# GpSimd's constants beside the last scores, the last batch's output in its own buffer, first weights loaded during the projection

## What is computed

```
x = x + layernorm(attention(layernorm(x)))      # x: 4 batches x 1024 tokens x 256, 16 heads of 16, rope on q and k
x = x + layernorm(moe(layernorm(x)))

attention: softmax(q k^T / 4) v, then out @ Wo.T + bo
moe:       dist = sqrt(max(|xs|^2 + |cent|^2 - 2 xs cent^T, 1e-12))     # 8 experts
           w, sel = top_k(dist, 2); w = softmax(w)
           out = sum over the two of w * ((silu(xs Wg + bg) * (xs W1 + b1)) W2 + b2)
```

## Time and profile before

| | us |
|---|---|
| median of 3 runs | 1444.86 |
| lowest and highest run | 1440.01, 1445.14 |
| profiled execution, its own time | 1442.97 |
| its span in the trace | 1441.1 |
| TensorE busy in the span | 1321.9 (92%) |
| VectorE, ScalarE, GpSimd busy | 1153.6, 942.0, 557.2 |

### The profile page before, as it was taken

The page is one execution under the profiler, slowest core; times in us unless marked ns, Lnnn a source line. Parts: engine busy times, 40 slices in busy tenths (PEclk is TensorE's granted clock), DMA queues, the critical chain, the costliest instruction groups (busy, mean ns, idle before and its releaser), DMA issues.

```text
span 1441.1 us, 27408 instructions
## 1 busy us (share of the span) xinstructions
PE 1321.9 (92%) x9553; PEld 793.2 (55%) x9554; DVE 1153.6 (80%) x1688; ACT 942.0 (65%) x1731; POOL 557.2 (39%) x473
## 2 busy tenths in 40 slices
PE   7999999999999999999999683699999999999980
PEld 4445333333333333333334451599999899899970
DVE  7989999999999999999930668477777667777765
ACT  4531888888888888888887561254555455455445
POOL 5670013040404023040450540355555455555545
PEclk9999999999999999999999885799999999999995
DMA  6875539647665757677225459665565656555646
GB/s 205 238 275 107 121 69 250 162 88 193 115 187 94 205 98 148 148 128 206 81 79 148 84 169 373 254 165 153 151 164 152 215 151 166 153 149 166 192 118 237
DMA packets 132293, 236.27 MB, mean 164 GB/s; under 512 B 56892, under 2 KB 93183, under 8 KB 130400
## 3 DMA queue, kind: packets, MB, share of 16 engines
q1 hardware_dynamic: 116288, 216.32, 53.9%
q0 software_dynamic: 15904, 18.66, 7.9%
HBM read 161.05 MB, written 79.50 MB: 167 GB/s over the span
## 4 chain that ended last, share of the span: by engine, by line
PE 75%; DVE 8%; DMA 6%; issue 4%; ACT 3%; POOL 3%; SPq 1%; POOLq 0%; DVEq 0%; ACTq 0%
PE psum L1601 21%; PE psum L1627 20%; PE psum L1776 15%; PE psum L1794 6%; DMA y_d<-sums,row_of 3%; PE psum L1796 3%; PE psum L1785 3%; PE psum L1613 2%; PE psum L1575 1%; DVE mx L1051 1%; ACT memory L1419 1%; POOL memory L976 1%; PE psum L1561 1%; DMA values<-xn_d,token_of 1%; PE psum L1758 1%
## 5 line engine op out<-in xcount | busy, mean ns | idle before, releaser
L1051 DVE TENSOR_REDUCE mx<-psum 128x1 f32<-128x1024 f32 x512 | 622.7, 1222 | 13.7 <-PE psum L1601 8.6
L1413 ACT ACTIVATE memory<-psum 128x512 f32<-128x512 f32 x1024 | 553.4, 600 | 63.9 <-PE psum L1613 1.4
L1613 PE MATMUL psum<-stack 50*128 50x512 f32 x1024 | 375.7, 446 | 0.0
L1601 PE MATMUL psum<-stack 48*128 48x512 f32 x1024 | 371.1, 443 | 2.5 <-DVE mx L1051 1.7
L1627 PE MATMUL psum<-memory,values 128*32 128x256 f32 x4096 | 326.3, 391 | 4.6
L1776 PE MATMUL psum<-w_parts,x_parts 128*128 x1278 | 284.8, 376 | 1.2 <-DVE x_parts L1281 1.2
L1601 PEld LDWEIGHTS psum<-stack 48*128 48x128 f32 x1024 | 150.4, 184 | 210.8 <-DVE mx L1051 168.4
L1776 PEld LDWEIGHTS psum<-w_parts,x_parts 128*128 128x128 f32 x1278 | 237.1, 190 | 23.7 <-issue 1.8
L954 POOL DMA_INDIRECT y_d<-sums,row_of x71 | 133.8, 1884 | 179.7 <-DVE sums L1303 149.6
L1490 ACT ACTIVATE sums<-psum,dots 128x256 f32<-128x256 f32 x71 | 33.8, 476 | 233.0 <-issue 118.7
L1627 PEld LDWEIGHTS psum<-memory,values 128*32 128x32 f32 x4096 | 81.9, 108 | 187.8 <-issue 106.6
(11 more groups left out here) (194 smaller groups left out, 1425.7 us busy)
## 6 DMA issues: line engine op xcount, KB each, us to landing
w_parts<-w_d SPq DMA_DIRECT2D x71, 768.0 KB
stack<-qk_scr SPq DMA_DIRECT2D x192, 128.0 KB, 6.0
w_d<-w_parts SPq DMA_DIRECT2D x6, 2736.0 KB, 8.1
w_parts<-w_d SPq DMA_DIRECT2D x6, 2736.0 KB, 14.9
qk_scr<-memory SPq DMA_DIRECT2D x16, 1024.0 KB, 4.5
raw<-in_w SPq DMA_DIRECT2D x16, 684.0 KB
ot_scr<-memory SPq DMA_DIRECT2D x16, 512.0 KB, 3.2
memory<-in_x SPq DMA_DIRECT2D x7, 1024.0 KB, 11.5
```

The costliest lines, as they stand in the source:

```text
L1051: dve.tensor_reduce(mx[:, r, a, t:t + 1], bank(4 + 2 * a, 2), AX, ALU.max, negate=True).then_inc(s_max, 1)
L1413: act.activation(pt[u % 4][:, j, :], bank((c + HG * u + n) % 3), ACT.Exp, scale=SC).then_inc(s_exp, 1)
L1601: ins = pe.matmul(bank(4 + 2 * a + half), qs[t3][at:at + QROWS, r, P * t:P * (t + 1)], ks[t3][at:at + QROWS, r, 512 * half:512 * (half + 1 ...
L1613: pe.matmul(bank((t3 + HG * u + n) % 3), ks[t3][at:at + MROWS, r, P * st:P * (st + 1)], qs[t3][at:at + MROWS, r, 512 * half:512 * (half + ...
```

## The change

- The fourth `ot` buffer. `OT_OF` is gone, each batch has a buffer, and that of batch 3 lies over `o_stage` and `v_stage` and the words behind them. Its loads no longer wait for `s_op`; the first waits until the values have been copied (`s_vg`) and the output is stored.
- SyncE's order. The last output is stored as soon as it is in `o_stage`, its sums are loaded next, then come all loads of batch 2 and batch 3, the latter no longer among the keeps. x2 is stored in four quarters behind keeps 3, 7, 11 and 15.
- The first weights. Load 5 moves into the last attention group, loads 0, 1 and 2 stand behind keeps 5, 9 and 13, each with a wait for the projections that free its place.
- GpSimd. Its constants wait for the weighing of all but the last two units, not for the last store. The halves of `norm_o` of batches 2 and 3 stand alone, before `add_y` 4, 6, 8 and 10, where both halves stood before 6 and 10.
- TensorE waits for the last copy of the output only before `turn_xn2(1)`, which writes the bank that held it.

```diff
--- before.py
+++ after.py
@@ -56,7 +56,6 @@
 Q_PART = [0, 0, 1]
 K_PART = [0, 1, 0]
 HEAD_ORDER = (1, 3, 0, 2)
-OT_OF = (0, 1, 2, 0)
 
 
 def steps(eng, count, stages, head=2):
@@ -188,6 +187,7 @@
         c.at = 16416
         ot = [c.take([2, KC, T]) for _ in range(2 + 1)]
         assert c.at == 24608 + stack_at
+        ot.append(weights[:, c.at:c.at + 2 * KC * T].rearrange("p (a k t) -> p a k t", a=2, k=KC))
         o_stage = c.take([T])
         v_stage = [c.take([ST, HG * D]) for _ in range(2)]
         assert c.at <= 32896
@@ -539,13 +539,11 @@
             sp.wait_ge(s_ot, 16 * HG * (b + 1))
             if b == 2:
                 sp.wait_ge(s_sp, BLOCKS * NG)
-            elif b == 3:
-                sp.wait_ge(s_op, 4)
             src = ot_scr[HG * b:HG * (b + 1), :, :].rearrange("(k x) (j s d) t -> s x j d k t", x=2, s=2, d=D)[0]
             for x in parts:
                 for j in range(HG):
                     at = 64 * x + D * j
-                    sp.dma_start(ot[OT_OF[b]][at:at + D, 0, :, :], src[x, j]).then_inc(s_otl[b % 2], 16)
+                    sp.dma_start(ot[b][at:at + D, 0, :, :], src[x, j]).then_inc(s_otl[b % 2], 16)
 
         def load_sums(sp, b):
 
@@ -563,13 +561,11 @@
             sp.wait_ge(s_rst, 16 * (b + 1))
             if b == 2:
                 sp.wait_ge(s_sp, BLOCKS * NG)
-            elif b == 3:
-                sp.wait_ge(s_op, 4)
             src = r_scr[b].rearrange("(k x j) t -> x j k t", x=2, j=HG)
             for x in parts:
                 for j in range(HG):
                     at = 64 * x + D * j
-                    sp.dma_start(ot[OT_OF[b]][at:at + D, 1, :, :], src[x, j].partition_broadcast(D)).then_inc(s_otl[b % 2], 16)
+                    sp.dma_start(ot[b][at:at + D, 1, :, :], src[x, j].partition_broadcast(D)).then_inc(s_otl[b % 2], 16)
 
         def load_raw(sp, n):
 
@@ -691,39 +687,38 @@
                                  zeros[:, :].rearrange("p (a d) -> p a d", a=1).to_broadcast([P, NT + 1, C])).then_inc(s_yc, 16)
                 elif g == 5:
                     load_wo(sp)
+                elif g == NG - 1:
+                    sp.wait_ge(s_wl, KC * E)
+                    load_w1(sp, 5)
 
             groups(sp, during)
             sp.wait_ge(s_sp, BLOCKS * (NG - 1))
             for m in range(4):
                 sp.dma_start(x2[:, 8 * m:8 * m + 8, :], x_v[:, 8 * m:8 * m + 8, :]).then_inc(s_x2l, 16)
+            store_o(sp, NG - 1)
+            load_sums(sp, B - 1)
             load_ot(sp, 2)
-            store_o(sp, NG - 1)
             load_inverses(sp, 2)
-            load_sums(sp, B - 1)
+            sp.wait_ge(s_vg, NG)
+            load_ot(sp, B - 1)
+            store_inverses(sp, B - 1)
+            load_inverses(sp, B - 1)
             def keep(u):
 
                 sp.wait_ge(s_one, u + 1)
                 sp.dma_start(xn2_d[2 * P * u:2 * P * (u + 1), :].rearrange("(a p) c -> p a c", p=P), xn2[u % 4]).then_inc(s_keep[u % 4], 16)
 
+            x2_kept = x2_d.rearrange("(n p) d -> p n d", p=P)
             for u in range(NT // 2):
-                if u == 2:
-                    store_inverses(sp, B - 1)
                 keep(u)
-                if 2 <= u < 6:
-                    (load_ot, load_inverses)[u // 2 - 1](sp, B - 1, (u % 2,))
-                if u == 7:
-                    sp.wait_ge(s_wl, KC * E)
-                    load_w1(sp, 5)
-                if u == 12:
-                    sp.wait_ge(s_vg, NG)
-                    sp.wait_ge(s_op, 12)
-                    load_w1(sp, 2)
-            sp.wait_ge(s_x2, NT // 2)
-            sp.dma_start(x2_d.rearrange("(n p) d -> p n d", p=P), x2).then_inc(s_x2s, 16)
-            sp.wait_ge(s_op, NT // 2)
-            for n in range(2):
-                load_w1(sp, n)
-            sp.wait_ge(s_x2s, 16)
+                if u % 4 == 3:
+                    sp.wait_ge(s_x2, u + 1)
+                    sp.dma_start(x2_kept[:, 2 * u - 6:2 * u + 2, :], x2[:, 2 * u - 6:2 * u + 2, :]).then_inc(s_x2s, 16)
+                if u in (5, 9, 13):
+                    n = (u - 5) // 4
+                    sp.wait_ge(s_op, 4 * n + 8)
+                    load_w1(sp, n)
+            sp.wait_ge(s_x2s, 64)
             sp.wait_ge(s_dd, 1)
             load_w1(sp, 3)
             sp.wait_ge(s_wc, 1)
@@ -849,11 +844,11 @@
             for r in range(PAIRS):
                 split_max(0, r)
 
-            def norm_o(b):
-
-                for half in range(2):
+            def norm_o(b, halves=(0, 1)):
+
+                for half in halves:
                     pool.wait_ge(s_otl[b % 2], 16 * 4 * HG * (b // 2 + 1))
-                    dims, inverses = [ot[OT_OF[b]][:, part, :, 512 * half:512 * (half + 1)] for part in range(2)]
+                    dims, inverses = [ot[b][:, part, :, 512 * half:512 * (half + 1)] for part in range(2)]
                     pool.tensor_tensor(dims, dims, inverses, ALU.mult).then_inc(s_div, 1)
 
             def split_weights(n):
@@ -885,7 +880,7 @@
             groups(pool, during)
 
 
-            pool.wait_ge(s_ot, 16 * NG)
+            pool.wait_ge(s_pv, UNITS * NG - 2)
             made = [0]
 
             def const(ins):
@@ -927,8 +922,8 @@
                 pool.tensor_tensor(both, both, yn[u % 2], ALU.add).then_inc(s_x2, 1)
 
             for u in range(NT // 2):
-                if u in (6, 10):
-                    norm_o(u // 4 + 1)
+                if u in (4, 6, 8, 10):
+                    norm_o(u // 4 + 1, (u % 4 // 2,))
                 add_y(u)
                 if u >= 3:
                     set_ones(u - 3)
@@ -1686,7 +1681,6 @@
 
 
             pe.wait_ge(s_wo, 48)
-            pe.wait_ge(s_oe, 2 * NG)
             pe.wait_ge(s_exp, BLOCKS * NG)
             pe.wait_ge(s_max, 2 * UNITS * NG)
 
@@ -1704,13 +1698,15 @@
                     dst = bank((4, 5, 0, 1)[u % 4])[:, C * a:C * (a + 1)]
                     pe.matmul(dst, ones_r[:, :], bias_rows, start=True, stop=False)
                     for k in range(KC):
-                        last = pe.matmul(dst, ot[OT_OF[u // 4]][:, 0, k, at + P * a:at + P * (a + 1)], w_o[:, k, :],
+                        last = pe.matmul(dst, ot[u // 4][:, 0, k, at + P * a:at + P * (a + 1)], w_o[:, k, :],
                                          start=False, stop=k == KC - 1)
                 last.then_inc(s_op, 1)
 
             def turn_xn2(u):
                 pe.wait_ge(s_xn2, 2 * u + 2)
                 after(pe, s_xn2t, u - 1)
+                if u == 1:
+                    pe.wait_ge(s_oe, 2 * NG)
                 for a in range(2):
                     for k in range(KC):
                         last = pe.transpose(bank((7, 3)[u % 2])[:, P * (KC * a + k):P * (KC * a + k + 1)],
```

## The result

The changed kernel takes 1446.9 us (median of 20 runs, 1441.31 to 1473.95) where the kernel before takes 1443.3 on the same chip. The ratio is 1.0022, 95% interval 1.0014 to 1.0029: some 3 us slower, by more than the measurement is uncertain, but within the 0.5% that the prediction called no change. It had said 1445.4, between 1437 and 1451. The profiled execution has a span of 1443.9 us, 2.8 longer than before. The highest of the 20 is of a disturbed execution, which the ratio leaves out; the profile of the experiment with all weight loads behind the loop is of another, so no time of it is read.

What follows compares the result with a forecast made beforehand. Bound by a ring of waits among VectorE, ScalarE and GpSimd, no engine full. Loop loss 866.9 + 1.5 - 864.03 = 4.4, less 2.0 gained behind it, is +2.4 on 1442.97: 1445.4 us, range 1437 to 1451.

Steps and rivals of the forecast that it cites:

- A0: Start of GpSimd's first add_y, after the earlier constants: 790.2 instead of 799.41, a gain of 9.2 us.
- The pieces and keep(0), the step said to count: SyncE's queue: loads of batches 2 and 3 land 1.0 us apart ahead of keep(0), landing at 826.1; ScalarE stands 13 us.
- A4: Start of GpSimd's fifth add_y, after batch 2's last piece at 806.9 and the norm_o half behind it: 809.3.
- The restart: GpSimd's additions in the loop, as the ring of waits between engines starts again: 1.6 us over the 3.65 pace.
- The halves: Each norm_o half on GpSimd holds VectorE's small offset operation, 3.65 becoming 4.77 us: 1.12 each, 4.5 for four.
- The first weight load: Load behind keep(5), landing in 9.5 us; ScalarE's norm_x2(10) waits for the next keep: 0.2 us lost.
- the nine steps: GpSimd from add_y(6) to add_y(15): nine steps of 3.65, 1.6 for the restart, 2.24 for two halves: 36.7 us.
- The weight load behind keep(13): ScalarE's norm_x2(14) waits for a keep behind a weight load, 1.3 us lost; the prediction has that load follow keep(9).
- The first gather: First gather of tokens after the loop, meeting a quiet queue: 2.0 us gained of 5.84, between 0 and 3.2.
- the first: Rival: kept rows don't bind in the loop, pieces landing 0.45 us apart instead of 1.0; 1428.5 us; 8 in 100.
- The second, overtaking: Rival: keep(0) overtakes transfers ahead in SyncE's queue, ScalarE released at 822.1, 4.0 us less; 1441.4 us; 12 in 100.
- The third, weight loads at 14.9: Rival: weight loads in the loop land in 14.9 us, not 9.5, and hold the keeps: +10.8, 1456.2 us; 8 in 100.

Runs made afterwards that it cites:

- the two experiments on the queue's order: Against the changed kernel: batch 3's loads in fours among the first keeps, 1432.73 us; only keep(0) ahead of batch 3's inverses loads, 1441.18 us.
- one keep ahead: Changed kernel with only keep(0) put ahead of the eight loads of batch 3's inverses: 1441.18 us, ratio 0.9992.
- the fillers: Changed kernel plus small unread matmuls in TensorE's idle times before transposes of pairs 13 and 14: 1445.82 us; on the quarters and split loads kernel, 1428.03 us.
- split loads: Kernel with batch 3's loads among the first keeps, each of the loop's three weight loads issued in two halves with a keep between: 1429.34 us, ratio 0.9898.
- quarters and split loads: Kernel with batch 3's loads among the first keeps, norm_o in quarters before add_y(4) to add_y(11), weight loads in halves: 1428.05 and, repeated, 1427.71 us.

## Why the prediction held, point by point

**The constants.** Right: A0 at 790.00, forecast 790.2.

**The pieces and keep(0), the step said to count.** Right in mechanism, and the two experiments on the queue's order show it. Too slow by 3.5 us: ScalarE was released at 822.57, forecast 826.1. The store of batch 3's inverses landed at 812.5 (the reload went out at 812.50), forecast 815.4. From the first piece's landing at 792.1 (788.1 + 4.0) that makes 24 intervals of 0.85 us, where the sum took 1.0 from the kernel before. In the kernel before, the store of the last output, four times a piece's size, lies among the pieces and was counted as one interval, but that is not shown to be the reason: the pace differs between executions of the same order. In the kernel with two weight loads behind the loop, whose queue is the same up to here, the reload went out at 815.73 and ScalarE was released at 825.75, where the forecast had 826.1; with one keep ahead the reload went out at 816.21, with the fillers at 813.57.

```profile
815.73 3.57 SPq L568 DMA_DIRECT2D memory<-r_scr  x8
```

So the profile of the changed kernel has the earliest reload of the four, which lie up to 3.7 us apart, and that is more than the 3 us that the change costs. What this spread comes of is open. ScalarE stood 11.0 us, forecast 13.

**A4.** 807.96 against 809.3, from the same pace.

**From pair 6 to the end of the loop.** 38.2 us (826.63 to 864.80) against 36.7 + 0.2. The restart cost 1.65 (831.93 - 826.63 - 3.65), forecast 1.6. The halves ahead of pairs 8 and 10 cost 1.12 each (836.70 - 831.93 = 4.77), exactly as taken; those ahead of pairs 4 and 6 lay beside longer waits. The first weight load cost 1.2 at pair 12's addition (853.66 - 848.77 - 3.65) where 0.2 had been counted. It landed in 10.7 us, not in 9.5. The end came out at 864.80 instead of 867.1 (866.9 and the 0.2): the release was 3.5 early, and the nine steps took 1.3 more than counted.

**The weight load behind keep(13).** 1.43 at pair 14, forecast 1.3.

**The first gather.** Right in sign, half in size: 0.9 gained (4.93 against 5.84), where 2.0 was taken between ends of 0 and 3.2. Most of the 5.84 was its own latency: in the changed kernel the DMA engines' share is 0.00 from 905 to 911 us, before the gather, and in the kernel before it is 0.94 to 1.00 from 906 to 912, beside it.

**What was not in the sum.** TensorE's clock in the last pair, 2.2 us. The working priced TensorE nowhere in its sum; behind the last pair the routing waits for it. The errors cancel in part: 1445.4 - 3.5 (the pieces) + 1.3 (the nine steps) + 0.1 (pair 14) + 1.1 (the gather) + 2.2 (the clock) = 1446.6, which is the +3.6 at the first transposes. The forecast came within 1.5 us of the median by terms that were off by up to 3.5. That it came so close is luck; that nearly nothing would be left of the 9.4 us, and where they would go, is not.

**The rivals.** The kept rows bound, so the first is out. The second, overtaking, is out by the keep that took 13.8 us. The third, weight loads at 14.9, is out: the three in the loop landed in 10.7, 9.9 and 12.9, of which the keeps behind the first two were waited for. What the prediction called a sign of being wrong, ScalarE standing twice more by 5 us, showed only as 1.36 and 1.43.

**What stays open.** What decides TensorE's clock at the last pair. Low in the changed kernel; high before, where it had been low for the pair ahead of it, and likewise with one keep ahead, where TensorE had stood 4.49 us before that pair; low without any stall in the split loads' profile, high in that of quarters and split loads with nearly the same idle times in the last two pairs; not held up by fillers. The Trainium skill, "TensorE: Matmul & The Clock Gate", Part 1, says that the number of matmuls at the low clock differs from run to run of one kernel. Here it differed between two kernels with nearly the same idle times, which fits but doesn't test it; with one profile of most kernels, nothing here separates an effect of the kernel from one of the execution. So of the 2.8 us between the two profiles, up to 2.2 may be the clock in these executions rather than the change, and what it was in the other runs isn't known. The gain lost with all weight loads behind the loop is open too.

## What to carry to other kernels

An engine's early start is worth what the next queue lets through: before moving loads ahead of a loop, list what stands behind them in their queue, and who waits for its first entries. A transfer that waits for a store of its own must not stand ahead of one that a loop needs every few microseconds; put among the loop's own transfers, the same loads no longer held ScalarE for 11 us, and the change that cost 0.2% gave 0.6%, and 1.0% with the weight loads in halves. Where small stalls alternate, removing one shows the next, so price the stretch as a chain of waits, and not each edit by itself.

## What the runs showed of the hardware

The pieces are slow for their size, and what stands behind them in the queue waits. 128 KB each into 16 partitions, they landed some 0.85 us apart, 154 GB/s. In that stretch all DMA engines count as busy (share 1.04 from 793 to 802 us), though they move only some 160 GB/s; with weight loads and keeps, which use all 128 partitions, stretches of the changed kernel with a share of 0.96 to 1.00 move 345 to 416. That it is the number of partitions, and not something else in the shape of these transfers, no run separates. The Trainium skill, "SBUF — State Buffer", section "Door 1: The DMA port swizzle", says that 16 partitions reach 4 of 16 ports and gives 104 GB/s for them; the rate here is above that, perhaps because two pieces in flight lie on different partitions; no run shows it. Alternating pieces from the two halves of the partitions was not tried.

A small transfer's landing is set by what is ahead of it and hardly by itself: 64 KB of inverses took 3.3 us at the median of the kernel before, 11.0 behind the pieces in the changed kernel, and 13.1, 15.3 and 15.5 in three other profiles with the same transfers ahead of it. Between two profiles, an early difference of 2.9 us became one of 5.3 at the end of the loop; TensorE's granted clock was 0.50 in the slower one, from 812 to 818 us, where the difference grew.
